# Delta rule: the right side ahead of the key products, three output transposes ahead of the last silu, the decays one slot sooner, and the last half product for the lower rows only

## The reference

```python
def step(S, inp):
    q_t, k_t, v_t, g_t, b_t = inp
    S = S * jnp.exp(g_t)[..., None, None]
    kv = jnp.einsum('bhk,bhkv->bhv', k_t, S)
    delta = (v_t - kv) * b_t[..., None]
    S = S + k_t[..., :, None] * delta[..., None, :]
    o = jnp.einsum('bhk,bhkv->bhv', q_t, S)
    return (S, o)
...
q = _causal_conv_silu(h @ Wq, conv_q_w)   # k and v alike
g = -jnp.exp(A_log) * jax.nn.softplus(h @ Wa + dt_bias)
beta = jax.nn.sigmoid(h @ Wb)
o = _rmsnorm(o, o_norm_w) * jax.nn.silu(gate)
x = x + o.reshape(b, t, VAL_DIM) @ Wo
x_out = jax.nn.gelu(_layernorm(x) @ W2 + b2) + x
```

## Time and profile before

| | |
|---|---|
| three runs | 4578.50, 4586.45 and 4582.89 us, median 4582.89 |
| profiled execution | 4581.29 us, of which the span of the trace is 4579.3 us |
| busy share of the span | PE 87%, DVE 54%, ACT 43%, POOL 24% |
| the delta rule's share | from about 2150 to about 4090 us of the span |

### The profile page before, as it was taken

How to read it: one execution, slowest core, us unless ns; L and a number is a source line. 1 busy time by engine, 2 the same in 40 slices (tenths; PEclk the granted TensorE clock), 3 DMA queues, 4 the chain that set the end, 5 groups by cost and what they waited for, 6 DMA issues and landing times. The chain is left out here.

```text
span 4579.3 us, 72621 instructions
## 1 busy us (share of the span) xinstructions
PE 3966.9 (87%) x23860; PEld 3077.2 (67%) x23860; DVE 2462.0 (54%) x5456; ACT 1990.2 (43%) x4069; POOL 1085.3 (24%) x1689
## 2 busy tenths in 40 slices
PE   5887788698999999993798888888888888769998
PEld 3555555377888888881576767676767677646666
DVE  7888888452222222224577777777777676421111
ACT  5655655111222222212466666666666566432222
POOL 0111111102222222212343333333333332200000
PEclk8888888799999999996799999999999999879999
DMA  1010010345555555552111111111111110011111
GB/s 34 29 42 28 28 42 20 75 135 179 183 183 183 184 183 185 183 170 68 39 42 40 43 41 42 42 42 38 42 43 42 42 42 25 20 51 55 55 55 46
DMA packets 220427, 345.91 MB, mean 76 GB/s; under 512 B 99956, under 2 KB 171380, under 8 KB 201972
## 3 DMA queue, kind: packets, MB, share of 16 engines
q1 hardware_dynamic: 196404, 271.69, 18.7%
q0 software_dynamic: 23760, 71.07, 4.9%
HBM read 275.56 MB, written 67.63 MB: 75 GB/s over the span
## 5 line engine op out<-in xcount | busy, mean ns | idle before, releaser
L525 ACT ACTIVATE moe_rel<-moe_fc 128x512 f32<-128x512 f32 x284 | 169.6, 597 | 798.5 <-PE moe_fc L490 798.5
L490 PE MATMUL moe_fc<-moe_xT,moe_win 128*128 128x256 f32 x2272 | 503.8, 380 | 1.5 <-issue 0.8
L501 PE MATMUL moe_o<-moe_wout,moe_hT 128*128 128x256 f32 x2272 | 502.0, 379 | 0.0
L490 PEld LDWEIGHTS moe_fc<-moe_xT,moe_win 128*128 128x128 f32 x2272 | 433.1, 191 | 60.8 <-issue 2.1
L501 PEld LDWEIGHTS moe_o<-moe_wout,moe_hT 128*128 128x128 f32 x2272 | 426.6, 190 | 54.8
L549 DVE TENSOR_TENSOR moe_hT<-moe_rel 128x512 f32<-128x512 f32 x284 | 196.7, 693 | 361.0 <-ACT moe_rel L525 361.0
L1776 DVE SCALAR_TENSOR_TENSOR gdr_y<-gdr_bank,gdr_cw,gdr_y 128x511 f32<-128x511 f32 (+2 forms) x384 | 287.5, 749 | 79.8 <-ACT gdr_y L2044 59.3
L2251 PE MATMUL gdr_bank<-gdr_hT,gdr_wqkv 128*128 128x512 f32 x512 | 261.7, 636 | 41.5 <-ACT gdr_qk L2059 24.6
L558 DVE COPY moe_osb<-moe_o 128x512 f32<-128x512 f32 x71 | 49.1, 692 | 424.9 <-PE moe_o L501 424.9
L723 DVE TENSOR_TENSOR ffn_z<-ffn_o,ffn_xres 128x512 f32<-128x512 f32 x32 | 20.6, 686 | 381.5 <-PE ffn_o L690 381.5
L679 PE MATMUL ffn_fc<-ffn_xT,ffn_win 128*128 128x512 f32 x512 | 224.5, 597 | 1.2 <-ACT ffn_xT L699 1.2
(11 more groups left out here) (391 smaller groups left out, 8584.6 us busy)
## 6 DMA issues: line engine op xcount, KB each, us to landing
moe_win<-in_moe_w SPq DMA_DIRECT2D x71, 1024.0 KB, 7.9
moe_wout<-in_moe_w SPq DMA_DIRECT2D x71, 1024.0 KB, 5.1
slots_out<-moe_osb POOLq DMA_DIRECT2D x71, 256.0 KB, 7.4
ffn_xin<-mixed_rows SPq DMA_DIRECT2D x17, 512.0 KB, 3.8
gla_xp<-in_xT_rows SPq DMA_DIRECT2D x16, 512.0 KB, 4.7
gla_xres<-in_x_rows SPq DMA_DIRECT2D x16, 512.0 KB, 3.9
token_rows<-gla_x POOLq DMA_DIRECT2D x16, 512.0 KB, 3.4
rt_W<-in_fc_b SPq DMA_DIRECT2D x32, 256.0 KB, 3.3
```

The lines of the kernel that those rows point to most:

```text
L490: ins = nc.tensor.matmul(fc_ps[j][:, m % 2, :], win[u][:, c, m * P:(m + 1) * P], xT[:, c, :], start=(c == 0), stop=(c == DT - 1))
L501: ins = nc.tensor.matmul(o_ps[u][:, t, :], hT[u][:, k, t * P:(t + 1) * P], wout[u][:, k, :], start=(k == 0), stop=(k == FT - 1))
L525: nc.scalar.activation(rel[:, j, :, :], fc_ps[j][:], ACT.Relu).then_inc(relu_done, 1)
```

## The change

Four edits:

1. DVE, slot 0: the right side `R` of chunk 2 (previous sequence) stands ahead of `products(0)`. PE had that order already.
2. Slot 9: three of the four output transposes, instead of two, stand ahead of the last `to_tokens` on PE, and likewise their copies on ACT ahead of the last `spread_out`.
3. `reach` on PE and `rates(1)` on ACT go from slot 12 to slot 11. On PE `reach` now stands ahead of `mix_out(1)`.
4. At the last level the half product `Y` is made, and copied, for the lower 64 rows only. The second product of that level reads Y against a part of `U` whose upper 64 rows are zero there.

```diff
+        rows_of = lambda lv: slice(0, P) if lv < LEVELS - 1 else slice(HP, P)
...
-                        if here and lv < 0:
-                            products(pair, b)
                         t, part = CHUNK_AT.get(slot, (None, None))
                         if t is not None and t >= 2 and past:
                             chunk(t, part, b - 1, w)
+                        if here and lv < 0:
+                            products(pair, b)
...
-                    done("Ye", n, copy(Y[i][:], bank[YZ[i]][:, 0:DH * HP].rearrange("p (h c) -> p h c", h=DH)))
+                    done("Ye", n, copy(Y[i][rows_of(lv), :, :], bank[YZ[i]][rows_of(lv), 0:DH * HP].rearrange("p (h c) -> p h c", h=DH)))
...
                         if past and slot == 9:
-                            turned_o(0, b - 1)
-                            turned_o(1, b - 1)
+                            for c in range(DH - 1):
+                                turned_o(c, b - 1)
                         if front and 2 <= slot <= NP_ + 1:
                             spread_out(slot - 2, b + 1)
                         if past and slot == 9:
-                            turned_o(2, b - 1)
-                            turned_o(3, b - 1)
+                            turned_o(DH - 1, b - 1)
...
+                        if front and slot == 11:
+                            rates(1, b + 1, w)
                         if front and slot == 12:
-                            rates(1, b + 1, w)
                             channels(0, b + 1, w)
...
-                        ins = mm(bank[YZ[i]][:, h * HP:(h + 1) * HP].rearrange("p (m n) -> p m n", n=half), nAT[:, i, h, :], first,
-                                 start=True, stop=True)
+                        ins = mm(bank[YZ[i]][rows_of(lv), h * HP:(h + 1) * HP].rearrange("p (m n) -> p m n", n=half),
+                                 nAT[:, i, h, rows_of(lv)], first, start=True, stop=True)
...
                         if past and slot == 9:
                             if here:
                                 pe.wait_ge(s["qd"], b * TT + TT)
-                            turn_o(0, b - 1)
-                            turn_o(1, b - 1)
+                            for c in range(DH - 1):
+                                turn_o(c, b - 1)
...
                         if past and slot == 9:
-                            turn_o(2, b - 1)
-                            turn_o(3, b - 1)
+                            turn_o(DH - 1, b - 1)
+                        if front and slot == 11:
+                            reach(b + 1)
                         if past and slot == 11:
                             mix_out(1, b - 1)
-                        if front and slot == 12:
-                            reach(b + 1)
```

## The result

The changed kernel takes 4576.69 us (median of 20 runs, 4563.78 to 4586.51) against 4585.98 us of the kernel before in the same series. The ratio is 0.9975, 95% interval 0.9964 to 0.9987: faster by 0.25%, about 11 us (the medians lie 9.3 us apart), where 30 were forecast. 4576.69 lies 0.7 us outside the range.

A forecast was written before the change was run, and what follows sets the result against it. First halves were taken as bound by a PE, ACT and DVE chain, second halves by PE and the blocks' round trip. 26 + 0 + 1 + 10 - 7 = 30 us off 4581.3 gave 4551 us, range 4522 to 4576.

The forecast's parts named there:

- the clock: First halves, slot 5: new waits of about 2.2 us cost two lost stretches for one, 7 us more.
- the delay of `nAT`: Slot 0, DVE: R's 1.13 us fits into a 2.23 us idle gap, so nAT and N0 are delayed by 0, at most 0.1.
- Edit 1, 26 us: Slots 0 to 6: R earlier gives a 1.9 us lead, DVE carries it to N1; 26 us over 14 periods.
- kind A: One of two alternating period types, 56.00 + 60.76 us; N1 forecast 1.7 us earlier in 8 full periods.
- kind B: The other alternating period type, 56.93 + 58.64 us; N1 forecast 2.1 us earlier in 6 full periods.
- the rival of the round trip: From slot 5 on PE decides, N1 does not follow, R's move gives little: 4568 to 4572 us; chance 0.13.
- the clock falls in slot 5: Rival: each lost stretch costs 5.7 us against 2 us gained; slower than before, 4618 us if in all 14; chance 0.12.
- Edit 2, 0 us: Slot 9: ACT's queue makes the same five copies and ends at the same time, so gain and loss are 0.
- Edit 3, 1 us: Slot 12: the wait for gam becomes one for ACT's copy; use 2 starts 0.2 us earlier, 1 us in all.
- Edit 4, 10 us: Slot 15: lower-row half products save 0.30 us per four, two groups, 0.6 us in 16 periods, 10 us.
- nothing hidden since PE has no wait there: Slot 15: the half products' saving of 0.6 us a period was taken to count in full.

The follow-up runs named there:

- e4: Changed kernel plus two 128x512 products on PE (results overwritten) in slot 5 ahead of the wait for the blocks; ratio to the kernel before 0.9916.
- e6: Kernel before with only R ahead of the key products, plus two overwritten 128x512 products ahead of the slot 5 wait; ratio 0.9920.
- e3: Kernel before with only the last level's half product cut to the lower rows; ratio 0.9968.
- e8: Kernel before with only the decays (reach, rates) a slot sooner; ratio 1.0001.
- e9: Kernel before with only three output transposes ahead instead of two; ratio 1.0013.
- e1: Kernel before with only R ahead of the key products; ratio 0.9988.
- e2: Changed kernel without the three transposes ahead; ratio to the kernel before 0.9967.
- e12: Changed kernel plus one overwritten 128x512 product on PE in slot 5 ahead of the wait for the blocks; ratio to the kernel before 0.9952.
- e13: Changed kernel, but behind the loop's jump DVE makes R between nAT and QD; ratio to the kernel before 0.9975.
- e15: As e6, but behind the loop's jump DVE makes R between nAT and QD; ratio to the kernel before 0.9908.
- e11: Kernel before with only R ahead, and chunk 3's due state and output products ahead of the slot 5 wait for the blocks; ratio 0.9955.

## Why the prediction was wrong, point by point

The forecast sign and the main mechanism were right and the size was not; three terms of the sum were mis-sized by about 6 us each: the clock, the delay of `nAT`, and edit 4.

**Edit 1, 26 us: mechanism right.** R fits into the gap, PE's wait for it is gone, the lead of about 2 us reaches slot 5, and where the clock holds N1 follows by 1.6 us (kind A) and 2.15 (kind B), against 1.7 and 2.1. So DVE decides N1, and the rival of the round trip falls: e4 and e6 have as late blocks and the full gain. At full clock (e4) it brings 23.6 us, 2.4 less than forecast, and the shortfall lies in periods 1 and 14. The forecast counted them as kind A, but before they have 52.24 and 53.11 us, and PE does not wait for the merge in slot 6 there; e4 has 52.78 and 53.09. The twelve others gain 24.2 us, against 22.8 forecast for them.

**The clock, "7 us more", is the first term that failed.** The prediction took two lost first halves for one, at 5.7 us each, from six waits of 2.2 us in slot 6. Measured, the clock falls behind the new wait in 10 of 14 periods. Against e4 with the fall just behind N0 of its period 12 taken out (760.8 - 1.7 = 759.1 us for the 14), that costs 780.0 - 759.1 = 20.9 us, 2.1 for each, because a fall lasts 3.4 or 6.8 us and DVE's lead absorbs part. What before lost in its two disturbed first halves (62.63 and 58.68 us, 5.7 + 1.8 above the others of kind B) is not lost again, so the net is 13.4 us instead of 7. These are two profiled executions. Without edit 1, e3, e8 and e9 lost 15, 4 and 5 us to falls in the first halves; with it and unfilled, e1 and e2 lost 28 and 27, with 11 and 12 falls behind slot 5. So the net is rather above 13 than below. The rival "the clock falls in slot 5", given 0.12, named the place, but it ended slower than before, since it priced each fall like the one long fall in the trace. Both the frequency and the price had been read off one disturbed period, and its 5.7 us hold two falls: the clock was low already behind PE's wait for R in slot 1, and 1.7 of the 5.7 us were lost before slot 5:

```profile
3581.31 1.13 PE L2315 MATMUL gdr_bank<-gdr_R,gdr_U 128*128 128x128 f32 x8 [2.59 <-DVE gdr_R L1886]
3582.27 3.42 PE L2296 MATMUL gdr_bank<-gdr_wg,gdr_hTg 128*128 128x512 f32 x4
```

The second row takes 1.88 us at full clock. The waits of slot 6 were taken for the same case as those in slot 5. They are not: in the four kernels without edit 1 the clock fell behind slot 6 in 5 of 24 periods of kind B, in the three with it and nothing in the wait behind slot 5 in 33 of 42. What makes the difference stays open. The length of the wait alone does not: in the changed kernel 2.24 us (period 4) lost the clock, 2.25 (6 and 10), 3.05 (3) and 3.20 (13) did not, and in e12 1.40 us did.

**"Its delay of `nAT` is 0" holds at 9 of 14 places.** At the five jumps DVE itself is late, R no longer fits into a gap in front of `nAT`, and it costs 1.28 us each, 6.4 us: the 1.13 us that the prediction named for "without that gap", at places where it did not look. The trace of before had a sign of it: in four of the five jumps N0 comes 5.3 to 5.6 us after the state product, and 4.87 us at every place without a jump, so there DVE, not PE, came last.

**Edit 2, 0 us: right.** `mix_out(0)` starts as long after N1. That all idle time ahead of it is now one piece of 3.16 us costs the clock of the product after it (mean 5.68 us against 4.96; e9 5.92 against 4.96; the kernels with edit 2 and nothing added in front have 5.55 to 5.92, those without it 4.96 to 5.37), which the prediction had not seen; the round trip hides most of it.

**Edit 3, 1 us: right within what can be told.** The wait in slot 12 is 2.42 us for ACT's copy, as foreseen.

**Edit 4, 10 us: half.** The half products cost what was forecast, 0.68 us for a group of four instead of 1.00:

```profile
3034.97 0.68 PE L2375 MATMUL gdr_bank<-gdr_T,gdr_nAT 128*64 128x64 f32 x8
```

But of the two groups in slot 15 the second's 0.3 us turns into the wait of 0.31 us for `Y`, since ACT needs 0.59 + 0.37 us for its two copies whatever PE saves. From slot 13 to N0 kind B has 30.21 to 30.23 us where nothing else disturbs it, and 30.53 before: 0.32 us, 16 x 0.32 = 5 us. e3, with this edit alone, has 30.20 to 30.22 there; e1, e6, e8 and e9, without it, 30.53 or 30.54. The error is "nothing hidden since PE has no wait there": there was none, but only by less than 0.3 us. Of the two statements that the prediction took from the Trainium skill (TensorE: Matmul & The Clock Gate, Step-by-step: what each phase is for), the trace agrees with the one that a weight load's time scales with its columns: a load of 64 columns takes 137 ns in the mean, one of 128 columns 220. The other, that throughput is "purely `N cycles`", does not give the time of these products, since each brings its own load: with the same 64 moving columns the group is faster by a third.

**The sum again.** In the 14 periods 30 us were to go, and 8.3 went. At full clock edit 1 gives 790.2 - 7.5 - 759.1 = 23.6 us, 2.4 less than its 26; the clock takes 13.4 instead of 7, which is 6.4 more; the jumps take 6.4; edit 4 gives 14 x 0.32 = 4.5 instead of 10, 5.5 less; edit 3's 1 us does not show. 2.4 + 6.4 + 6.4 + 5.5 + 1 = 21.7. For the first halves the closing proves nothing, since the clock's term is what e4 leaves over. For the second halves it is partly luck: single ones scatter by 2 to 4 us with the clock. What runs have shown by changing it alone is the clock's part (e4, e6) and edit 4's 0.32 us a period (e3). The jumps' part is read from the timelines: e13 and e15 show that R's place moves N0 there, at four of five jumps, and do not win it back.

## What to carry to other kernels

Where a saving only moves an engine sooner to a transfer that does not move, look at what the new wait does to TensorE's clock behind it, and try to fill the wait with work that is due anyway; here that more than doubled the gain (0.9937 against 0.9975), though one kernel so filled (e11) still lost the clock in five first halves. Check a "free" gap at every place where the code runs, the loop's jump among them, and before a term is written as "nothing hidden", work out how much later the next engine in line is. One disturbed period in a trace gives neither the frequency nor the price of the next.

## What the runs showed of the hardware

- Two added 128x512 products on PE, 1.88 us of work without use, shortened each first half by 1.4 us (e4 against after): the clock stayed at its higher level for the 3 to 7 us behind the wait.
- Waits of nearly the same length, 2.24 and 2.25 us, ended with the clock lost in one period and kept in another. A wait of 1.40 us lost it (e12, period 10), one of 3.20 us kept it (after, period 13).
- At the loop's jump of the changed kernel DVE stands idle for 4.6 to 5.2 us in four of five cases, PE for 1.4 to 2.3 us, both put down to "issue". What they wait for the profile does not show.
- Four fp32 products with 64 weight columns instead of 128, at 64 moving columns, take 0.68 us instead of 1.00.
